# Moving the rounding and the DMAs of fifteen weight tiles inside the first batch of a two-layer kernel

## The chip, the cores and the metric

The kernel runs on one core of a Trainium2 chip. The metric is the device time of one launch in microseconds (us). Before the change it is 2076.19 us, the median of three runs (2070.89 to 2077.12). The engines are TensorE (PE; its weight loads are PEld), VectorE (DVE), ScalarE (ACT), GpSimd (POOL) and SyncE (SP, which only issues DMAs here).

## The reference

Eight sequences of 512 tokens with 256 channels go through two layers. In each, a normalised input feeds an attention and a gated feed-forward net, and their product is added to the input. All is in fp32.

```python
x = L0_attn_x                                   # (8, 512, 256)
xn = _layernorm(x)
s = L0_attn(xn)    # 16 heads of 16, 4 key heads, bias -slope*sqrt(i-j), causal
g = _silu(L0_ffn(xn))                           # silu(x W1') * (x W3'), Walsh-Hadamard, W2'
x = x + s * g
xn = _layernorm(x)
s = L1_attn(xn)    # differential attention, 32 softmaxes of width 8, rms norm
g = _silu(L1_ffn(xn))                           # shared expert and 8 experts of width 176, top 2
x = x + s * g
```

## The kernel before

**Batches and units.** One batch is one sequence; there are B = 8, one after the other. Within a batch, layer 0 is four *units* (u = 0 to 3, four heads each) and layer 1 is eight (u = 4 to 11). A unit goes through eleven *packs* of scores (`SCORE_PACKS`): for each, PE makes the scores (line 535), DVE adds the distance bias to six of the eleven in layer 0 (`dve_bias`, line 812), and ACT takes the exponentials (`act_exps`, line 696). POOL masks and multiplies two of the four heads (`pool_distances`, lines 826 and 829), for key tiles kt = 0, 1, 2 in turn. Then PE multiplies by v (`pe_pv`, line 551).

**The maxima of the next unit.** Between the packs of unit u, PE also makes the scores of unit u + 1 (`pe_max_pack`, lines 501 and 508) and DVE takes their row maxima (`dve_maxima`, lines 794 and 797). When all eleven are done, PE transposes them (line 514), ACT copies them as `mneg` (line 676) and SP writes them into a row of the q ring. `mneg` is the mark by which the prediction counts units.

**Up tiles.** The feed-forward weights come in 22 *up tiles*. Layer 0 uses tiles 0 to 7, layer 1 tiles 8 to 21. For each, PE runs 12 matmuls into two banks (line 452, a gate half and a linear half of 6 each), ACT takes a tanh (line 706), and DVE folds it (`dve_gate_half`, line 837, and `dve_linear_half`, line 847). `TILE_IN` gives the tile that is finished inside a unit and `TILE_AFTER` the one that is finished at its end. The matmuls of a linear half wait until the linear half of the tile before has left its bank (`s_h`). In units 1 and 2 the last six matmuls, four ahead of line 514 and two behind it (`UP_BEHIND`), are such a linear half; the one they wait for is `TILE_IN[u]`, folded by DVE at pack 9. After unit 3 come the down products (line 616).

**Late tiles.** Each weight is used as a sum of two rounded parts: high (rounded to fp32r) and low (the remainder). A rounded tile is kept in the DRAM image `up_img`, from which SP and ACT load it when it is due. Seven tiles are made in a setup block ahead of the batches. The fifteen others, 7 to 21, are made in the first batch only (b = 0), during its four layer-0 units, by the table `LATE_TILES` (4, 4, 4 and 3 tiles). Each goes through four steps in one of four places in SBUF (`late_pairs`, tile t in place (t - 7) mod 4: two in `hbuf`, one in `xn`, one in `x`):

- `pool_late_in` (line 960): POOL issues the load of 256 KB, after the store of the tile that had the place before has landed (`s_lout`);
- `act_late_high` (line 965): ACT rounds, after the load has landed (`s_lin`);
- `dve_late_low` (line 970): DVE subtracts, after the ACT step (`s_lhi`);
- `pool_late_out` (line 976): POOL issues the store of 512 KB into `up_img`, after the DVE step (`s_llo`).

**What sets the order.** It is written out by hand: each engine runs its own program in order (`act_batch`, `dve_batch`, `pool_batch`), and counted semaphores join them. An instruction that waits holds everything behind it on its engine. In the first batch, before the change, ACT and DVE do the roundings of a unit behind all its packs, and POOL issues the loads of a unit's tiles between its kt = 0 and kt = 1 work of that same unit. The tiles of unit 0 are loaded at its start.

Of the kernel before, what the change touches and what calls it, by code (L numbers as in the profile page):

```python
# [36 lines left out]
UNITS = (4, 8)  # L37
# [80 lines left out]
def gated_layers_kernel(nc, x_in, w0_qk, w0_v, w0_o, w_up, w0_down, w1_qk, w1_v, w1_o, w1_down,  # L118
                        w1_gate, gate_bias, lambdas, subln, c_ident, c_hadamard, c_dist, c_causal, out):
    with ExitStack() as ctx:  # L120
# [835 lines left out]
        def pool_late_in(pool, t):  # L956
            n, s = divmod(t - UP_EARLY, LATE_STAGES)
            if n:
                pool.wait_ge(s_lout[s], so_far(s_lout[s], 16 * n))
            nc.gpsimd.dma_start(late_pairs[s][:, 1, :], w_up[t]).then_inc(s_lin[s], 16)  # L960

        def act_late_high(act, t):
            n, s = divmod(t - UP_EARLY, LATE_STAGES)
            act.wait_ge(s_lin[s], so_far(s_lin[s], 16 * (n + 1)))
            nc.scalar.copy(late_pairs[s][:, 0, :].bitcast(F32R), late_pairs[s][:, 1, :]).then_inc(s_lhi, 1)
# [209 lines left out]
        with nc.Block() as block:  # L1175
# [220 lines left out]
            def act_batch(act, b, more_batches):  # L1396
                def unit(u):
                    for i in range(PACKS):
                        if i == PACKS - 1 and u < UNITS[0] - 1:
                            act_max_copy(act, u + 1)  # L1400
                        act_exps(act, u, i)
                        if i == 8 and U0[1] <= u < U_ALL - 1:
                            act_tanh(act, TILE_AFTER[u])
                        if i == PACKS - 1 and U0[1] <= u < U_ALL - 1:
                            act_max_copy(act, u + 1)
                        if i == 1 and u not in U0:
                            act_pv_copy(act, u - 1)
                        if i == 1 and u == 0:
                            act_tanh(act, 0)
                        if i == (4 if u < UNITS[0] - 1 else 6) and u in TILE_IN:  # L1410
                            act_tanh(act, TILE_IN[u])
                        if u == U_ALL - 1 and i in (6, 9) and more_batches:
                            act_turn(act, 0, (6, 9).index(i))
                        if u == U_ALL - 1 and i == 7:
                            act_tanh(act, TILE_AFTER[u])
                    if u < UNITS[0]:
                        act_tanh(act, TILE_AFTER[u])
                    if u < UNITS[0] and not b:
                        for t in LATE_TILES[u]:
                            act_late_high(act, t)  # L1420
                    if u < UNITS[0] - 1:
                        if u:
                            act.wait_ge(s_pm2, so_far(s_pm2, 3 * u))
                        act_strips(act, u + 1)
                    if last_of_layer(u):
                        act_pv_copy(act, u)

                for u in range(UNITS[0]):
                    unit(u)
                act_tanh_down(act, 0, 0)  # L1430
                act_o_turn(act, 0)
                act_turn(act, 1, 0)
                act_tanh_down(act, 0, 1)
                act_turn(act, 1, 1)
                act_project(act, 1, 0)
                act_project(act, 1, 1)
                act.wait_ge(s_rp, so_far(s_rp, 1))
                nc.scalar.activation(rt[:, 0].rearrange("p t e -> p (t e)"), MX[1][:, 0:NT * NE], ACT.Tanh,
                                     scale=0.5).then_inc(s_rsg, 1)
                act_v(act, 1)  # L1440
                act_tanh(act, FRONT_TILES[0])
                act_project(act, 1, 2)
                act_tanh(act, FRONT_TILES[1])
                up_load(act, FRONT_TILES[1] + 2)
                act_project(act, 1, 3)
                act_tanh(act, FRONT_TILES[2])
                up_load(act, FRONT_TILES[2] + 2)
                act.wait_ge(s_rT, so_far(s_rT, 1))
                nc.scalar.copy(gT[:], MISC[0:NE, :]).then_inc(s_rTc, 1)
                act_tanh(act, FRONT_TILES[3])  # L1450
                up_load(act, FRONT_TILES[3] + 2)
                act_max_copy(act, UNITS[0])
                for j in FRONT_TILES[4:]:
                    act_tanh(act, j)
                    up_load(act, j + 2)
                for u in range(UNITS[0], U_ALL):
                    unit(u)
                if not more_batches:
                    act_tanh_down(act, 1, 0)
                    act_o_turn(act, 1)  # L1460
                    act_tanh_down(act, 1, 1)
                    return

                for i in range(3):
                    act_project(act, 0, i)
                act_v(act, 0)
                act.wait_ge(s_rm, so_far(s_rm, 1))
                act_strips(act, 0)
                act_tanh_down(act, 1, 0)
                act_o_turn(act, 1)  # L1470
                act_tanh_down(act, 1, 1)
                act.wait_ge(s_mrow[1], so_far(s_mrow[1], 16 * (U_ALL - 1)))
                act_max_copy(act, 0)
# [7 lines left out]
            def dve_batch(dve, b, more_batches):  # L1481
                def unit(u):
                    more = not last_of_layer(u)
                    late = layer_of(u) == 0
                    for i in range(PACKS):
                        if late and i in BIAS_PACKS and i < PACKS - 1:
                            dve_bias(dve, u, i)
                        if more:
                            dve_maxima(dve, u + 1, i)
                        if i == 1 and u == 0:  # L1490
                            dve_gate_half(dve, 0)
                        if i == 2 and u == 0:
                            dve_linear_half(dve, 0)
                        if late and more and u in TILE_IN and i == 5:
                            dve_gate_half(dve, TILE_IN[u])
                        if late and more and u in TILE_IN and i == 9:
                            dve_linear_half(dve, TILE_IN[u])
                    if u in TILE_IN and not more:
                        dve_gate_half(dve, TILE_IN[u])
                    if late:  # L1500
                        dve_bias(dve, u, PACKS - 1)
                    if u in TILE_IN and not more:
                        dve_linear_half(dve, TILE_IN[u])
                        dve_normalise(dve, u - 1)
                    dve_gate_half(dve, TILE_AFTER[u])
                    dve_linear_half(dve, TILE_AFTER[u])
                    if more and u not in U0:
                        dve_normalise(dve, u - 1)
                    if late and not b:
                        for t in LATE_TILES[u]:  # L1510
                            dve_late_low(dve, t)
                    if last_of_layer(u) and u < U_ALL - 1:
                        dve_normalise(dve, u)

# [100 lines left out]
            def pool_batch(pool, b, more_batches):  # L1615
                for u in range(UNITS[0]):
                    if u == 0 and not b:
                        for t in LATE_TILES[0]:
                            pool_late_in(pool, t)
                        for img in (q_img, k_img):  # L1620
                            nc.gpsimd.dma_start(img[1][:, 3:32:4, :], qring[1][:, 0, 0:2, :].bitcast(F32)).then_inc(s_pad, 16)
                    for kt in range(NT - 1):
                        pool_distances(pool, u, kt)
                        if u and kt == 0 and not b:
                            for t in LATE_TILES[u]:
                                pool_late_in(pool, t)
                    if u == 1 and not b:
                        pool.wait_ge(s_pad, so_far(s_pad, 32))
                        nc.gpsimd.dma_start(k_img[1][3:32:4, 31, :], kring[0][MROW:MROW + 1, 0:1, :].bitcast(F32)
                                            .to_broadcast([1, 8, T])).then_inc(s_ones, 16)  # L1630
                    if not b:
                        for t in LATE_TILES[u]:
                            pool_late_out(pool, t)
                    if u == UNITS[0] - 1 and not b:
                        for l in (0, 1):
                            nc.gpsimd.dma_start(wo[l][:], (w0_o, w1_o)[l]).then_inc(s_wo[l], 16)
# [119 lines left out]
```

## Time and profile before

| what | value |
|---|---|
| median of three runs | 2076.19 us |
| the profiled execution | 2082.67 us |
| its span | 2080.9 us |
| PE, DVE, ACT, POOL busy | 94%, 68%, 42%, 33% |
| first batch, layer 0 | from 54.63 to 124.67 us |
| second batch, layer 0 | from 319.70 to 379.28 us |

The span is the time between the first and the last instruction in the trace; the profiled execution's time is 1.8 us longer. Engine times are counted from the start of the span. A busy share is an average over the whole span and says little about one batch; for the fifteen tiles only the stretch from 54 to 128 us counts, and the second batch, which has the same four units without late tiles, is what it can be held against.

### The profile page before, as it was taken

Reading aid. Unit: us, or ns where it says so; the run is one execution under the profiler, and the core shown is the slowest. Engines: PE = TensorE matmul, PEld = TensorE weight load, DVE = VectorE, ACT = ScalarE, POOL = GpSimd, SP = SyncE. Lnnn points to the kernel's source line nnn. Section 1 sums busy time; section 2 is a strip of 40 time slices with the busy share of each in tenths; the row PEclk is TensorE's granted clock in tenths of the full one; section 3 lists DMA queues with packets and bytes.
Section 4 is the critical chain, followed back from the end, with each engine's and each line's share of the span. In section 5 each row is a group of like instructions: output and inputs, shape, how many; then the busy total and the mean of one; then the engine's idle time right before and its main releaser. Section 6 shows DMA issues by size and latency. Waiting matters only on the chain.

```text
span 2080.9 us, 33061 instructions
## 1 busy us (share of the span) xinstructions
PE 1955.8 (94%) x11618; PEld 1434.5 (69%) x11618; DVE 1406.1 (68%) x3474; ACT 880.2 (42%) x1753; POOL 683.5 (33%) x846
## 2 busy tenths in 40 slices
PE   5889999999999999999999999999999989999998
PEld 3566676766767667686676766767677766767666
DVE  6847758477575775757766676666766567675773
ACT  3534624345252452515524264243543436333462
POOL 2633413243142441414414143133332334232341
PEclk8999999999999999999999999999999999999999
DMA  8647332262322524234242442415332163421630
GB/s 265 213 144 245 100 101 61 72 208 83 102 77 97 172 73 118 71 128 147 63 112 81 161 128 64 106 63 185 118 89 68 62 200 115 103 61 42 204 101 16
DMA packets 105261, 240.46 MB, mean 116 GB/s; under 512 B 16700, under 2 KB 26940, under 8 KB 104840
## 3 DMA queue, kind: packets, MB, share of 16 engines
q1 hardware_dynamic: 85080, 173.44, 27.8%
q0 software_dynamic: 14256, 43.94, 6.8%
q10 hardware_dynamic: 5760, 20.97, 3.0%
q8 instruction: 93, 1.52, 0.3%
q14 instruction: 72, 0.59, 0.1%
HBM read 179.67 MB, written 57.82 MB: 114 GB/s over the span
## 4 chain that ended last, share of the span: by engine, by line
PE 75%; DVE 12%; DMA 5%; issue 3%; ACT 1%; POOL 1%; DVEq 0%; ACTq 0%; POOLq 0%; SPq 0%
PE bank L452 22%; PE bank L616 15%; PE bank L535 11%; PE bank L501 11%; PE bank L551 8%; DVE bank L794 4%; DMA qring<-mneg 4%; PE bank L637 3%; DVE nmax L797 3%; PE bank L508 2%; PE bank L561 2%; PE bank L514 1%; DVE probs L812 1%; PE bank L463 1%; DVE xn L746 1%
## 5 line engine op out<-in xcount | busy, mean ns | idle before, releaser
L452 PE MATMUL bank<-xnT,upring 128*128 128x512 f32 (+1 forms) x2208 | 713.5, 405 | 1.4 <-DVE hbuf L837 1.4
L794 DVE CUSTOM_DVE_ANT_0 bank<-bank,mask_strip 128x512 f32<-128x512 f32 (+1 forms) x768 | 479.0, 635 | 197.6 <-PE bank L501 195.6
L696 ACT ACTIVATE probs<-bank 128x512 f32<-128x512 f32 (+1 forms) x720 | 388.2, 555 | 282.8 <-PE bank L535 256.6
L452 PEld LDWEIGHTS bank<-xnT,upring 128*128 128x128 f32 x2208 | 405.4, 194 | 60.4 <-DVE hbuf L837 9.2
L501 PE MATMUL bank<-kring,qring 127*128 127x128 f32 (+3 forms) x1280 | 379.5, 350 | 23.0 <-DVE nmax L794 14.7
L535 PE MATMUL bank<-qring,kring 128*128 128x512 f32 (+1 forms) x880 | 358.2, 411 | 40.8 <-DMA qring<-mneg 19.3
L616 PE MATMUL bank<-wdown,hbuf 128*128 128x256 f32 x1408 | 324.4, 380 | 0.0
L501 PEld LDWEIGHTS bank<-kring,qring 127*128 127x128 f32 x1280 | 227.1, 193 | 114.5 <-DVE nmax L794 62.6
L616 PEld LDWEIGHTS bank<-wdown,hbuf 128*128 128x128 f32 x1408 | 263.4, 190 | 35.5 <-issue 1.7
L535 PEld LDWEIGHTS bank<-qring,kring 128*128 128x128 f32 x880 | 169.1, 194 | 128.8 <-issue 44.9
L1662 POOL TENSOR_SCALAR_AFFINE_SELECT probs<-probs 128x512 f32<-128x512 f32 x200 | 128.3, 642 | 369.1 <-ACT probs L696 368.7
L797 DVE TENSOR_REDUCE nmax<-bank 128x2 f32<-128x512 f32 (+1 forms) x288 | 199.0, 691 | 51.7 <-PE bank L508 42.9
L551 PE MATMUL bank<-probs,v 128*17 128x384 f32 (+3 forms) x2368 | 207.3, 452 | 4.1 <-POOL probs L829 3.6
L837 DVE SCALAR_TENSOR_TENSOR hbuf<-tb,bank 128x512 f32<-128x512 f32 x176 | 120.2, 683 | 88.9 <-ACT tb L706 88.9
L826 POOL TENSOR_SCALAR_AFFINE_SELECT probs<-probs 128x256 f32<-128x256 f32 x64 | 26.6, 416 | 421.0 <-ACT probs L696 421.0
L847 DVE SCALAR_TENSOR_TENSOR hbuf<-hbuf,bank 128x512 f32<-128x512 f32 x176 | 120.6, 685 | 28.0 <-PE bank L452 15.0
L829 POOL TENSOR_TENSOR probs<-probs,shared 128x1024 f32<-128x1024 f32 x64 | 135.7, 2121 | 5.3
L706 ACT ACTIVATE tb<-bank 128x512 f32<-128x512 f32 x176 | 104.3, 593 | 74.9 <-PE bank L452 74.9
L696 ACT ACTIVATE probs<-probs 128x512 f32<-128x512 f32 (+1 forms) x160 | 93.6, 587 | 91.2 <-DVE probs L812 91.2
L551 PEld LDWEIGHTS bank<-probs,v 128*17 128x17 f32 x2368 | 57.6, 97 | 102.7 <-issue 73.3
L1602 POOL TENSOR_TENSOR hbuf<-hbuf,gring 128x512 f32<-128x512 f32 x88 | 113.7, 1292 | 33.2 <-DMA gring<-gate_img 28.7
L713 ACT ACTIVATE tb<-bank 128x512 f32<-128x512 f32 x32 | 19.1, 597 | 244.2 <-PE bank L616 244.2
(165 smaller groups left out, 2309.4 us busy)
## 6 DMA issues: line engine op xcount, KB each, us to landing
upring<-up_img SPq DMA_DIRECT2D x136, 512.0 KB, 4.0
upring<-up_img ACTq DMA_DIRECT2D x40, 512.0 KB, 5.6
q_img<-probs SPq DMA_DIRECT2D x32, 512.0 KB, 3.3
kring<-k_img SPq DMA_DIRECT2D x64, 256.0 KB, 3.0
qring<-q_img SPq DMA_DIRECT2D x32, 384.0 KB, 4.7
qring<-q_img SPq DMA_DIRECT2D x192, 64.0 KB, 2.0
q_img<-probs SPq DMA_DIRECT2D x32, 256.0 KB, 4.0
k_img<-probs SPq DMA_DIRECT2D x16, 512.0 KB, 5.7
```

Of the source, the lines that this page charges most:

```text
L452: last = nc.tensor.matmul(out_ap, part_a(a, pa, k), part_b(b, pb, k), start=(n == 0), stop=(n == len(steps) - 1))
L501: last = nc.tensor.matmul(bk[:, (g - g0) * w:(g - g0 + 1) * w], q_of(u)[0:MROW, g, qt * P:(qt + 1) * P], k_of(u)[0:MROW, 0:w], start=True, ...
L535: nc.tensor.matmul(SC[n % 2][:, 0:heads * w].rearrange("p (g n) -> p g n", g=heads), k_of(u)[:, kt * P:(kt + 1) * P], q_of(u)[:, g0:g0 + h ...
L551: last = nc.tensor.matmul(PV[32 * g:32 * g + DV + 1, kt * P:T], v[l][:, kt, hv, :], probs_of(u, kt)[:, g, :], start=(kt == 0), stop=(kt == ...
L616: last = nc.tensor.matmul(FB[tt // 2][:, (tt % 2) * C:(tt % 2 + 1) * C], hbuf[:, j, tt * P:(tt + 1) * P], wdown[l][:, j, :], start=(j == 0 ...
L696: nc.scalar.activation(pr, pr if biased else scores, ACT.Exp, scale=scale).then_inc(s_exp, 1)
L794: nc.vector.tensor_tensor_reduce(scores, scores, mask_strip[:, T - w:T], 1.0, -BIG, ALU.add, ALU.max, nmax[:, u % 2, g0, qt:qt + 1]).then_ ...
L797: nc.vector.tensor_reduce(nmax[:, u % 2, g0:g0 + heads, qt], MX[n % 2][:, 0:heads * w].rearrange("p (g n) -> p g n", g=heads), AX.X, ALU.m ...
L829: nc.gpsimd.tensor_tensor(pr[:, :, 0:w], pr[:, :, 0:w], estrip[:, u % 2, :, 0:w], ALU.mult).then_inc(s_pm2, 1)
L837: nc.vector.scalar_tensor_tensor(hbuf[:, layer_tile(j)[1], :], tb[:], 1.0, FB[0][:], ALU.add, ALU.mult).then_inc(s_gu, 1)
L847: nc.vector.scalar_tensor_tensor(h, h, 0.5, FB[1][:], ALU.mult, ALU.mult).then_inc(s_h, 1)
L1662: nc.gpsimd.affine_select(pr, pr, [[0, G4], [1, P]], ALU.is_ge, 0.0, base=0, channel_multiplier=-1).then_inc(s_pm, 1)
```

## The change

Only the first batch is touched. The same fifteen loads, roundings and stores are done, in the same places in SBUF.

- ACT: in unit u, the k-th late tile is rounded right behind the exponentials of pack 5 + k, and no longer behind the unit.
- DVE: the k-th late tile is subtracted right behind the maxima of pack 6 + k, and no longer behind the unit.
- POOL: the stores of unit u stay behind its kt = 2 work, and the loads for unit u + 1 follow them at once, ahead of the kt = 0 work of unit u + 1. Before, they stood behind that work.

```diff
@@ act_batch, unit(u)
                         act_exps(act, u, i)
+                        if u < UNITS[0] and not b and 5 <= i < 5 + len(LATE_TILES[u]):
+                            act_late_high(act, LATE_TILES[u][i - 5])
...
                     if u < UNITS[0]:
                         act_tanh(act, TILE_AFTER[u])
-                    if u < UNITS[0] and not b:
-                        for t in LATE_TILES[u]:
-                            act_late_high(act, t)
@@ dve_batch, unit(u)
                         if more:
                             dve_maxima(dve, u + 1, i)
+                        if late and not b and 6 <= i < 6 + len(LATE_TILES[u]):
+                            dve_late_low(dve, LATE_TILES[u][i - 6])
...
                     if more and u not in U0:
                         dve_normalise(dve, u - 1)
-                    if late and not b:
-                        for t in LATE_TILES[u]:
-                            dve_late_low(dve, t)
@@ pool_batch
                     for kt in range(NT - 1):
                         pool_distances(pool, u, kt)
-                        if u and kt == 0 and not b:
-                            for t in LATE_TILES[u]:
-                                pool_late_in(pool, t)
...
                     if not b:
                         for t in LATE_TILES[u]:
                             pool_late_out(pool, t)
+                        if u < UNITS[0] - 1:
+                            for t in LATE_TILES[u + 1]:
+                                pool_late_in(pool, t)
```

DVE in unit 1, packs 7 to 10, before the change (L812 is a bias, L794 and L797 are maxima, L847 the linear half of tile 2):

```order
L812 SCALAR_TENSOR_TENSOR probs<-dist,bank 128x384
L794 ISA bank,nmax<-bank,mask_strip 128x384
L794 ISA nmax 128x1
L797 TENSOR_REDUCE nmax<-bank 128x2
L812 SCALAR_TENSOR_TENSOR hbuf<-dist,bank 128x256 x2
L797 TENSOR_REDUCE nmax<-bank 128x2
L847 SCALAR_TENSOR_TENSOR hbuf<-hbuf,bank 128x512
L797 TENSOR_REDUCE nmax<-bank 128x4
```

The same place on DVE after the change, from the end of pack 6 (L970 is the subtraction of a late tile):

```order
L970 TENSOR_TENSOR hbuf<-hbuf 128x512
L812 SCALAR_TENSOR_TENSOR probs<-dist,bank 128x384
L794 ISA bank,nmax<-bank,mask_strip 128x384
L794 ISA nmax 128x1
L970 TENSOR_TENSOR hbuf<-hbuf 128x512
L797 TENSOR_REDUCE nmax<-bank 128x2
L970 TENSOR_TENSOR xn<-xn 128x512
L812 SCALAR_TENSOR_TENSOR hbuf<-dist,bank 128x256 x2
L797 TENSOR_REDUCE nmax<-bank 128x2
L970 TENSOR_TENSOR x<-x 128x512
L847 SCALAR_TENSOR_TENSOR hbuf<-hbuf,bank 128x512
L797 TENSOR_REDUCE nmax<-bank 128x4
```

All four subtractions now stand ahead of the linear half and of the last maxima of the unit; units 0 and 2 have the same pattern.

POOL between units 2 and 3 before the change (L976 stores, L960 loads, L826 and L829 the two steps of `pool_distances`):

```order
L976 DMA up_img<-hbuf 128x1024 x2
L976 DMA up_img<-xn 128x1024
L976 DMA up_img<-x 128x1024
L826 AFFINE_SELECT probs<-probs 128x2x128
L829 TENSOR_TENSOR probs<-probs,shared 128x1024
L960 DMA hbuf<-in_w_up 128x512 x2
L960 DMA xn<-in_w_up 128x512
L826 AFFINE_SELECT probs<-probs 128x2x128
L829 TENSOR_TENSOR probs<-probs,shared 128x2x384
```

And after it:

```order
L976 DMA up_img<-hbuf 128x1024 x2
L976 DMA up_img<-xn 128x1024
L976 DMA up_img<-x 128x1024
L960 DMA hbuf<-in_w_up 128x512 x2
L960 DMA xn<-in_w_up 128x512
L826 AFFINE_SELECT probs<-probs 128x2x128
L829 TENSOR_TENSOR probs<-probs,shared 128x1024
L826 AFFINE_SELECT probs<-probs 128x2x128
L829 TENSOR_TENSOR probs<-probs,shared 128x2x384
```

The loads, each of which waits for a store to land, have moved from between kt = 0 and kt = 1 to ahead of both.

## Rows read from the trace of the kernel before

**Rows 1.** The page's first line.

```profile
span 2080.9 us, 33061 instructions
```

**Rows 2.** Chain of waits, 50 to 160 us: start, us, what.

```profile
106.56 6.49 DMA up_img<-hbuf
...
115.67 1.81 POOL probs L829
```

**Rows 3.** PE by 1 us: length, busy (instructions), granted clock, DMA share, GB/s.

```profile
116.00:117.00 1.00, 0.00 (x0) 0.67 0.98 397
...
122.00:123.00 1.00, 1.00 (x3) 0.50 0.00 0
123.00:124.00 1.00, 1.00 (x8) 0.92 0.00 0
```

**Rows 4.** ACT, the mneg copies, first batch, then second: start, us, instruction, [idle before].

```profile
68.00 0.27 ACT L676 ACTIVATE mneg<-bank 16x128 fp32r<-16x128 f32 x1 [1.10 <-PE bank L514]
...
84.68 0.27 ACT L676 ACTIVATE mneg<-bank 16x128 fp32r<-16x128 f32 x1 [1.95 <-PE bank L514]
...
101.66 0.27 ACT L676 ACTIVATE mneg<-bank 16x128 fp32r<-16x128 f32 x1 [1.93 <-PE bank L514]
...
333.69 0.27 ACT L676 ACTIVATE mneg<-bank 16x128 fp32r<-16x128 f32 x1 [1.42 <-PE bank L514]
...
348.50 0.27 ACT L676 ACTIVATE mneg<-bank 16x128 fp32r<-16x128 f32 x1 [1.93 <-PE bank L514]
...
363.75 0.27 ACT L676 ACTIVATE mneg<-bank 16x128 fp32r<-16x128 f32 x1 [1.92 <-PE bank L514]
```

**Rows 5.** PE at the end of unit 3, first batch, then second.

```profile
117.62 1.48 PE L551 MATMUL bank<-probs,v 128*17 128x384 f32 x8 [3.62 <-POOL probs L829]
119.03 4.93 PE L452 MATMUL bank<-xnT,upring 128*128 128x512 f32 x12
...
124.67 3.72 PE L616 MATMUL bank<-wdown,hbuf 128*128 128x256 f32 x16
...
375.54 3.04 PE L452 MATMUL bank<-xnT,upring 128*128 128x512 f32 x12
...
379.28 3.72 PE L616 MATMUL bank<-wdown,hbuf 128*128 128x256 f32 x16
```

**Rows 6.** DVE, the late subtractions behind unit 0.

```profile
71.00 1.28 DVE L970 TENSOR_TENSOR hbuf<-hbuf 128x512 fp32r<-128x512 f32 x2
...
73.41 0.69 DVE L794 CUSTOM_DVE_ANT_0 bank<-bank,mask_strip 128x512 f32<-128x512 f32 x1
```

**Rows 7.** DVE at the end of unit 1's packs.

```profile
82.58 0.68 DVE L847 SCALAR_TENSOR_TENSOR hbuf<-hbuf,bank 128x512 f32<-128x512 f32 x1
83.18 0.68 DVE L797 TENSOR_REDUCE nmax<-bank 128x4 f32<-128x512 f32 x1
```

**Rows 8.** Waits, 54 to 128 us: engine, line, for whom: total, times, longest.

```profile
PEld bank L452 <- DVE hbuf L847: 0.8, 2, 0.4
```

**Rows 9.** DVE and PE in unit 0.

```profile
64.79 0.69 DVE L797 TENSOR_REDUCE nmax<-bank 128x2 f32<-128x512 f32 x1 [0.75 <-PE bank L508]
...
66.16 1.48 DVE L797 TENSOR_REDUCE nmax<-bank 128x2 f32<-128x512 f32 x2
...
67.69 0.28 PE L514 MATMUL bank<-ident,nmax 128*16 128x128 f32 x1
```

**Rows 10.** Loads (line 960), then stores (line 976): time from issue to landing.

```profile
DMA to landing us min/median/max: 3.1/4.4/5.4
...
DMA to landing us min/median/max: 3.4/6.3/8.2
```

**Rows 11.** ACT and POOL, end of unit 2 and unit 3.

```profile
97.79 0.58 ACT L696 ACTIVATE hbuf<-bank 128x512 f32<-128x512 f32 x1
...
109.23 0.85 ACT L696 ACTIVATE probs<-bank 128x384 f32<-128x384 f32 x2
...
105.95 1.15 POOL L976 DMA_DIRECT2D up_img<-hbuf  x2 [3.36 <-DVE hbuf L970]
```

## The prediction, made before the changed kernel was run

> **What bounds the kernel now.** The page's head gives the span, 2080.9 us [rows 1]. The profiled execution took 2082.67 us, 6.5 us above the median of the three runs, 2076.19; I sum against the profiled execution and carry the difference over to the median unchanged. What the measurement can tell from no change is about 0.3%, 6.2 us.
>
> I then set the first batch's layer 0 beside the second's, which does the same work without late tiles. The marks are the copies of mneg, one per unit, and the start of the down products. From the mneg of unit 0 to that of unit 1 it is 84.68 - 68.00 = 16.68 us in the first batch and 348.50 - 333.69 = 14.81 in the second; to that of unit 2 it is 16.98 against 15.25 [rows 4]. From there to the down products it is 124.67 - 101.66 = 23.01 against 379.28 - 363.75 = 15.53 [rows 4, 5]. So the late tiles cost 1.87 + 1.73 + 7.48 = 11.1 us behind the first mneg. That is the most that this change could give back, 0.53% of the launch.
>
> The 7.48 us are read from the chain of waits. It goes through a store of unit 2's tiles for 6.49 us and then to POOL's kt = 1 work, which starts at 115.67 [rows 2]. POOL issues unit 3's loads between kt = 0 and kt = 1, each load waits for a store, and so kt = 1 is late: PE idles 3.62 us for it [rows 5]. Behind the idle time the granted clock falls to one half, 1.2 of 2.4 GHz, at about 116.3 (a third of that microsecond is at the old level), and comes back at about 123.2 [rows 3]. The twelve matmuls in it take 4.93 us against 3.04 in the second batch [rows 5]. The rest is shorter waits of the same kind, and the subtractions that still run when unit 3 starts.
>
> **The change part by part.**
>
> *Subtractions on DVE, units 0 to 2.* Four take 73.41 - 71.00 = 2.41 us [rows 6], 0.60 each. They go away behind the unit, where the next unit's first maxima now start as soon as PE has them, as in the second batch. They come in ahead of the unit's last maxima. In unit 1 DVE runs its last rows back to back, 82.58 and 83.18 [rows 7], and PE's weight loads for tile 3's linear half already wait for the linear half of tile 2 on DVE, 0.4 us each time [rows 8]. Both stand behind all four subtractions now, so line 514 and the mneg move by the full 2.41 us. Unit 1 is then the second batch's 14.81 + 2.41 = 17.22 us, 0.54 more than before. Unit 2 is 15.25 + 2.41 = 17.66, 0.68 more. The change loses there: more is put into the packs than leaves the seam, since of the 2.41 us only 1.87 and 1.73 were ever on the path there, the rest ran while PE was busy anyway.
>
> In unit 0 DVE has slack: it idles 0.75 us at 64.79 and the last two maxima end at 66.16 + 1.48 = 67.64 [rows 9]. With the four subtractions that is 67.64 + 2.41 - 0.75 = 69.3, less some 0.2 us of small gaps, 69.1. Line 514 was at 67.69 [rows 9] and is then 1.4 us later, so the first mneg is at 69.4. Bounds for the 2.41 us in the packs: nothing, if PE has other work wherever DVE is late; or 4 x (0.6 + 0.7) = 5.2, if every rounding on ACT and its subtraction run one after the other with DVE standing. I take 2.41, since ACT waits for DVE in front of most of its packs and so is ready first.
>
> *POOL.* The stores need only the last subtraction and kt = 2. In unit 2 the exponentials of pack 8 were at 97.79 [rows 11]; I put them at some 98.5 (its packs start half a microsecond earlier, and two subtractions stand ahead). POOL's kt = 2 is a little shorter than its kt = 1, whose multiplication alone is 1.81 us [rows 2]; with 2 us for it, the stores go out from about 101 in place of 105.95 [rows 11]. A store lands 6.3 us after its issue in the median and a load 4.4 us [rows 10]. Unit 3's loads are then issued from 107.3 and the first is in at 111.7. ACT wants it after pack 5: mneg of unit 2 at 104.3 (below) plus what that took before, 109.23 + 0.85 - 101.66 = 8.4, less the 0.9 us that this stretch lost to the subtractions, 111.8. So it is just in time. POOL's kt = 0 starts at about 109, close to where it was, but kt = 1 follows it at once, by about 112 and long before PE wants it. The 3.62 us and the fall of the clock go. For the loads of units 1 and 2 there is more room, since ACT wants them seven microseconds into the unit and the stores leave at the end of the unit before.
>
> The Trainium skill (DMA: Bandwidth & Descriptors, section on the anatomy of one DMA on the SWDGE path) fits a GpSimd-issued transfer with 2.0 us plus the bytes at 436 KB per us. My estimate from that page for three stores in flight is 2.0 + 3 x 1.2 = 5.6 us, a little shorter than the row's median, and would leave the forecast as it is.
>
> *Queued behind the new waits.* On POOL the waits for landed stores now hold kt = 0 too, for which PE waits at the seventh pack of unit 3. On ACT the wait for a load holds the exponentials of packs 6 to 8, and with them PE's next scores. SP issues the same transfers in the same order; its loads of tiles 7 and on wait for stores that land earlier than before. The last three stores and the output weights leave POOL earlier too and are wanted only in the down products.
>
> *Unit 3.* It takes no maxima, so DVE and ACT have idle time. Three subtractions are 1.8 us; between nothing and all of it is lost, I take half, 0.9 us. From mneg to down products that is 15.53 + 0.9 = 16.43 in place of 23.01, 6.58 less.
>
> **Sum.** mneg of unit 0 at 68.00 + 1.4 = 69.4; unit 1 at 69.4 + 17.22 = 86.6; unit 2 at 86.6 + 17.66 = 104.3; down products at 104.3 + 16.43 = 120.7, against 124.67. In terms: +1.4 + 0.54 + 0.68 - 6.58 = -4.0 us. Nothing behind moves against the down products. The span becomes 2076.9, the profiled execution 2078.7, the median 2072.2.
>
> **The rivals.**
>
> *A: the packs hide more.* If half of the 2.41 us is hidden in units 0 to 2, 3 x 1.2 = 3.6 us more come back: 7.6 in all, 2068.6. For it: PE runs a pack ahead of DVE and has up matmuls to fill in. Against it: rows 7 and 8 show no room at the end of units 1 and 2.
>
> *B: the transfers are late.* With the slowest store and load, 8.2 and 5.4 us [rows 10], unit 3's first load is in at 101 + 13.6 = 114.6, and ACT stands 2.8 us. The gain is 1.2 us, 2075.0. For it: these slowest ones were in this very stretch, with SP's loads beside them. Against it: the stores now go out before SP's loads.
>
> *C, the other side: the clock falls in units 1 and 2.* PE has run out of up matmuls at the end of the packs and now waits about 2 us for the linear half and the last maxima, with shorter waits ahead. If the granted clock then halves in both units for as long as it did in rows 3, 123.2 - 116.3 = 6.9 us, and PE has work throughout, each costs half of that, 3.4 us. The sum is -4.0 + 6.8: slower by 2.8 us, 2079.0. It decides from about 2 us per unit on. For it: rows 3 show such a fall. Against it: there PE stood for 3.62 us, and here it has work ahead of the wait and behind it. The Trainium skill (TensorE: Matmul & The Clock Gate, section on what's actually happening) says that the clock follows how busy TensorE has been of late; by that, several waits could add up to what one long one does, and rival C would be likelier than the single row makes it.
>
> *D: nothing moves.* The orders of the engines do change, so this needs gains and losses to cancel by chance, 2076.2; it lies between B and C.
>
> **How the numbers follow.** Forecast with its neighbourhood (gain 2.5 to 5.5 us) 0.5; A 0.17; B and D 0.21; C 0.12. The measured medians scatter: the three runs shown lie 6 us apart, which is half as much again as the forecast gain. The range reaches from A to between B and C, with a microsecond of scatter: 2067.5 to 2077.5; only C and the far end of A are left out. Faster by over 0.3% needs 6.2 us, so A or good luck in the medians: 0.21. Slower by over 0.3% needs worse than C: 0.04. Within 0.3%: 0.75.
>
> **What would show it.** In the profile after: mneg at about 69.4, 86.6 and 104.3 and down products at about 120.7; periods of units 1 and 2 half a microsecond longer than before; no wait of PE for POOL's line 829 in unit 3, and full clock from there to the down products; stores of unit 2's tiles from about 101; waits of ACT's line 965 for loads near zero. The forecast is wrong if the periods of units 1 and 2 shrink (A), if ACT or POOL stand for DMAs in unit 3 by more than a microsecond (B), or if the clock drops between 84 and 108 us (C).

## The result: slower, 2086.24 us against the 2072.2 forecast

| | before | after |
|---|---|---|
| median, 5 runs each on one chip | 2074.19 us (2070.89 to 2077.12) | 2086.24 us (2083.35 to 2092.51) |
| ratio | | 1.0065 [1.0051, 1.0079] |
| the profiled execution | 2082.67 us | 2089.81 us |
| first batch's layer 0, first scores to down products | 70.04 us | 80.87 us |

The loss lies in the stretch that was changed (the last row of the table; *stretch* stands for it from here on): 10.8 us more there, against 12 us in the medians. Behind the down products the profiled execution takes 1952.2 us, where before takes 1956.2; over all the profiles below this part lies between 1947.8 and 1960.8 us, so a profile is compared by its stretch, and a launch by its median. Each kernel has one profile, the kernel before a second one, with a stretch of 68.86 us in place of 70.04; differences of a microsecond between stretches say nothing.

The copies of mneg on ACT in the kernel after, the rows that answer to [rows 4]:

```profile
70.66 0.27 ACT L676 ACTIVATE mneg<-bank 16x128 fp32r<-16x128 f32 x1 [1.82 <-PE bank L514]
...
94.18 0.27 ACT L676 ACTIVATE mneg<-bank 16x128 fp32r<-16x128 f32 x1 [3.20 <-PE bank L514]
...
115.60 0.27 ACT L676 ACTIVATE mneg<-bank 16x128 fp32r<-16x128 f32 x1 [2.83 <-PE bank L514]
```

Unit 1 takes 23.52 us in place of 16.68 and unit 2 21.42 in place of 16.98; 17.22 and 17.66 were forecast. Unit 3 is shorter than before, but not by what was forecast:

```profile
122.25 0.47 PE L535 MATMUL bank<-qring,kring 128*128 128x512 f32 x1 [3.51 <-DMA qring<-mneg]
...
132.14 3.05 PE L452 MATMUL bank<-xnT,upring 128*128 128x512 f32 x12 [0.48 <-DVE hbuf L837]
```

This is PE in unit 3 after, and answers to [rows 5]: the twelve matmuls take 3.05 us, so the clock is whole, and no wait for POOL's line 829 stands in the unit. In its place stands a wait that did not exist before, at the unit's first scores, for the row of maxima that SP writes from mneg (line 426). PE's waits of after, 54 to 137 us, from the same view as [rows 8], show what is new:

```profile
PE bank L535 <- DMA qring<-mneg: 8.1, 3, 3.5
...
PE bank L535 <- DVE probs L812: 4.2, 5, 1.2
PE bank L452 <- DVE hbuf L847: 3.8, 2, 1.9
```

**The first cause: the row of maxima is late.** It is 8 KB. Before, it landed 1.8 us after its issue in all three units; PE had the last packs' products with v to do meanwhile and never waited. Line 426 before:

```profile
DMA to landing us min/median/max: 1.8/1.8/1.8
```

From the chain of waits of after:

```profile
70.96 5.61 DMA qring<-mneg
...
94.47 5.19 DMA qring<-mneg
...
115.89 6.22 DMA qring<-mneg
```

What moved ahead of it stands in POOL's rows of after:

```profile
69.08 1.14 POOL L976 DMA_DIRECT2D up_img<-hbuf  x2
70.20 0.55 POOL L976 DMA_DIRECT2D up_img<-xn  x1
70.72 0.54 POOL L976 DMA_DIRECT2D up_img<-x  x1
72.53 0.55 POOL L960 DMA_DIRECT2D hbuf<-in_w_up  x1 [1.27 <-DMA up_img<-hbuf]
```

```profile
up_img<-x POOLq DMA_DIRECT2D x1, 512.0 KB, 6.1
```

The last row is of the DMA view of 69 to 79 us (size, us to landing). The four stores of 512 KB are issued in the two microseconds ahead of the row. The last of them lands at 70.72 + 6.1 = 76.8, and the row at 76.57, together with it. In units 1 and 2 it is the same: last store 99.5 and 121.9, row 99.66 and 122.11. Before, they stood behind the unit's roundings and so always behind the row. The Trainium skill (DMA: Bandwidth & Descriptors, section on queues, rings and completion order) has the DMA engines take turns between the queues packet by packet; by that alone a small row on SP's queue should wait for little more than a packet. The rows above show more than that: the row arrives only with the last of the 2 MB. The same section of the Trainium skill says that the write which signals a transfer's end lands only after every earlier write of its DMA engine, across its queues. This could hold the row back as well; no run here tells whether its data or its signal is late.

**The second cause: the subtraction stands while POOL works.** DVE, then POOL, in unit 1 of after:

```profile
85.27 1.63 DVE L970 TENSOR_TENSOR hbuf<-hbuf 128x512 fp32r<-128x512 f32 x1
87.77 0.68 DVE L970 TENSOR_TENSOR hbuf<-hbuf 128x512 fp32r<-128x512 f32 x1
88.97 0.67 DVE L970 TENSOR_TENSOR xn<-xn 128x512 fp32r<-128x512 f32 x1
90.83 0.98 DVE L970 TENSOR_TENSOR x<-x 128x512 fp32r<-128x512 f32 x1
```

```profile
84.52 1.84 POOL L829 TENSOR_TENSOR probs<-probs,shared 128x768 f32<-128x768 f32 x1
89.00 0.91 POOL L826 TENSOR_SCALAR_AFFINE_SELECT hbuf<-hbuf 128x256 f32<-128x256 f32 x1 [2.65 <-ACT hbuf L696]
90.00 1.27 POOL L829 TENSOR_TENSOR hbuf<-hbuf,shared 128x512 f32<-128x512 f32 x1
```

POOL's multiplication ends at 84.52 + 1.84 = 86.36 and the first subtraction at 86.90, 0.54 later. The next one of POOL ends at 91.27 and the last subtraction at 91.81, again 0.54 later. So DVE does next to nothing of these subtractions, which take 0.68 us alone, before POOL is done. It goes the other way too: POOL's line 826 at 89.00 takes 0.91 in place of 0.41 us, and a subtraction has begun just before it, at 88.97. The Trainium skill (SBUF — State Buffer, section on the two separate sides) states this rule: a DVE operation with two inputs in SBUF and a GpSimd operation that reads SBUF take one pair of ports in turn, each for its whole length. The trace agrees: all seven subtractions that start while POOL computes end 0.54 to 0.55 us behind it. The biases with one operand in a bank keep their length: the one of 128x384 at 84.33, under POOL's multiplication, takes 0.55 us, and the one at 86.83, with POOL idle, 0.54.

**The clock** falls twice between the marks of units 0 and 2: at about 76.1, in the 3.34 us that PE stands for the row, and at about 93.2, less than 1 us behind PE's wait of 1.88 us for tile 2's linear half. PE by 1 us in after, columns as in [rows 3]:

```profile
75.00:76.00 1.00, 0.00 (x0) 1.00 1.04 240
76.00:77.00 1.00, 0.30 (x1) 0.57 1.03 361
77.00:78.00 1.00, 1.00 (x3) 0.50 0.90 320
...
93.00:94.00 1.00, 1.00 (x5) 0.61 1.02 410
94.00:95.00 1.00, 1.00 (x4) 0.50 0.88 328
```

**What they add up to.** The stretches of after, mneg to mneg: length, busy time of each engine, granted clock.

```profile
55.03:70.66 15.63, 12.99 (x41) 8.34 (x43) 14.81 (x34) 7.91 (x15) 12.31 (x15) 0.78 0.52 180
70.66:94.18 23.52, 17.02 (x87) 10.73 (x87) 16.94 (x40) 10.82 (x22) 12.71 (x17) 0.91 0.63 193
94.18:115.60 21.42, 16.97 (x91) 10.51 (x92) 17.00 (x39) 10.70 (x22) 11.52 (x14) 0.94 0.55 198
115.60:135.90 20.30, 15.20 (x110) 8.32 (x108) 11.80 (x23) 11.18 (x22) 12.48 (x15) 1.00 0.67 238
```

Unit 1 is 6.30 us over its forecast: 3.34 for the row, 0.95 + 0.30 for two subtractions that stand (1.63 and 0.98 against 0.68), and 0.09 x 23.52 = 2.1 by the clock, 6.7 in all. Unit 2 is 3.76 over: 1.27 for the row, some 1.2 again for two subtractions, and 0.06 x 21.42 = 1.3. Unit 3 is 3.87 over, 3.51 of it for the row. These sums are read from one trace; the experiments test them.

### The profile page after: what moved, and what is told of

Same layout as the page of the kernel before. It is cut to its first block, busy times and chain, and to the rows that moved or that the text cites. A ratio compares the mean times of both kernels' runs of the same rounds, so it can differ in the third digit from the quotient of the medians.

```text
span 2088.1 us, 32972 instructions
## 1 busy us (share of the span) xinstructions
PE 1952.5 (94%) x11529; PEld 1431.8 (69%) x11618; DVE 1410.3 (68%) x3474; ACT 879.9 (42%) x1753; POOL 684.8 (33%) x846
## 4 chain that ended last, share of the span: by engine, by line
PE 74%; DVE 13%; DMA 5%; issue 3%; ACT 1%; POOL 1%; ACTq 0%; DVEq 0%; POOLq 0%; SPq 0%
PE bank L452 22%; PE bank L616 15%; PE bank L535 10%; PE bank L501 9%; PE bank L551 8%; DMA qring<-mneg 4%; DVE bank L794 4%; PE bank L508 4%; DVE nmax L797 3%; PE bank L637 3%; PE bank L561 2%; PE bank L514 1%; DVE probs L812 1%; PE bank L463 1%; DVE xn L746 1%
## 5 line engine op out<-in xcount | busy, mean ns | idle before, releaser
L794 DVE CUSTOM_DVE_ANT_0 bank<-bank,mask_strip 128x512 f32<-128x512 f32 (+1 forms) x768 | 478.5, 634 | 206.2 <-PE bank L501 204.2
L797 DVE TENSOR_REDUCE nmax<-bank 128x2 f32<-128x512 f32 (+1 forms) x288 | 198.7, 690 | 48.5 <-PE bank L508 39.7
L826 POOL TENSOR_SCALAR_AFFINE_SELECT probs<-probs 128x256 f32<-128x256 f32 x64 | 26.5, 414 | 427.8 <-ACT probs L696 427.8
L829 POOL TENSOR_TENSOR probs<-probs,shared 128x1024 f32<-128x1024 f32 x64 | 136.9, 2138 | 5.3
L847 DVE SCALAR_TENSOR_TENSOR hbuf<-hbuf,bank 128x512 f32<-128x512 f32 x176 | 120.5, 685 | 26.5 <-PE bank L452 13.4
L706 ACT ACTIVATE tb<-bank 128x512 f32<-128x512 f32 x176 | 104.3, 592 | 69.6 <-PE bank L452 69.6
L812 DVE SCALAR_TENSOR_TENSOR probs<-dist,bank 128x128 f32<-128x128 f32 (+2 forms) x256 | 105.4, 446 | 27.8 <-PE bank L535 27.2
```

What stands on the lines that cost most here:

```text
L794: nc.vector.tensor_tensor_reduce(scores, scores, mask_strip[:, T - w:T], 1.0, -BIG, ALU.add, ALU.max, nmax[:, u % 2, g0, qt:qt + 1]).then_ ...
L797: nc.vector.tensor_reduce(nmax[:, u % 2, g0:g0 + heads, qt], MX[n % 2][:, 0:heads * w].rearrange("p (g n) -> p g n", g=heads), AX.X, ALU.m ...
L812: last = nc.vector.scalar_tensor_tensor(probs_of(u, kt)[:, g, :], dist[:, 0:w], -SLOPES[4 * u + g] / EXP_SCALE[0], SC[n % 2][:, (g - g0) * ...
L829: nc.gpsimd.tensor_tensor(pr[:, :, 0:w], pr[:, :, 0:w], estrip[:, u % 2, :, 0:w], ALU.mult).then_inc(s_pm2, 1)
L847: nc.vector.scalar_tensor_tensor(h, h, 0.5, FB[1][:], ALU.mult, ALU.mult).then_inc(s_h, 1)
```

## The experiments

**Row first.** POOL waits for the row to land before it issues the stores.

```diff
+                        if u < UNITS[0] - 1:
+                            pool.wait_ge(s_mrow[1], so_far(s_mrow[1], 16 * (u + 1)))
                         for t in LATE_TILES[u]:
                             pool_late_out(pool, t)
```

> The changed kernel, but in units 0 to 2 POOL waits for the landing of the next unit's maxima row before it issues the unit's stores. Theory 1 (the 8 KB row lands 5.2 to 6.2 us after its issue in place of 1.8 because the stores were issued just ahead of it and fill the DMA engines): the row lands in 1.8 us again, PE's waits of 3.3 to 3.5 us for it go, with the low clock behind the first; about 10 us faster than the changed kernel, near 2076 us or level with the kernel before. Rival (the row is late for another reason, and the in-pack roundings on DVE are what costs): the row stays late or its landing is not worth more than 3 us, time above 2082 us.

Measured: 2102.39 us against 2077.0, ratio 1.0121 [1.0099, 1.0144]; stretch 93.90 us. The row is back to 1.8 us in every unit, and yet this is the slowest kernel of all, 26 us above its expectation. Stores that leave later make the loads behind them late, and these hold ACT, five times and 18.0 us in all, and behind ACT PE, inside the packs:

```profile
81.81 0.62 ACT L965 CAST hbuf<-hbuf 128x512 fp32r<-128x512 f32 x1 [5.41 <-DMA hbuf<-in_w_up]
```

The expectation took it that the loads had room. They have none: with the roundings in the packs, stores, loads and row all want the same few microseconds between two units. The granted clock is low for much of this too, 0.83, 0.76 and 0.75 in units 1 to 3.

**Roundings alone.** The loads go back behind the kt = 0 work.

```diff
                         pool_distances(pool, u, kt)
+                        if u and kt == 0 and not b:
+                            for t in LATE_TILES[u]:
+                                pool_late_in(pool, t)
...
-                        if u < UNITS[0] - 1:
-                            for t in LATE_TILES[u + 1]:
-                                pool_late_in(pool, t)
```

> The changed kernel with the loads back behind kt = 0 of their own unit; the stores leave as early as in the changed kernel. Theory 1 (stores delay the row): row still lands after 4 to 6 us and the time stays within 4 us of the changed kernel's 2086. Rival (the loads that follow at once are what the row queues with): row back near 1.8 us and 8 us or more faster than the changed kernel.

Measured: 2097.34 us, ratio 1.0093 [1.0076, 1.0110]; stretch 87.04 us. The row's landing, over the three units, with no load issued near it:

```profile
DMA to landing us min/median/max: 4.0/5.1/5.2
```

So it is in the main the stores that delay it; the loads behind them, which after has and this kernel has not, add 0.4 to 1.2 us in the same unit. The time missed its expectation, 2082 to 2090 us: the loads come late for ACT, which stands 6.7 us for four of them, and the clock reads 0.81, 0.89 and 0.80 in units 1 to 3.

**POOL's order alone.** The opposite half: the kernel before with the loads moved, the roundings left behind the units.

```diff
-                        if u and kt == 0 and not b:
-                            for t in LATE_TILES[u]:
-                                pool_late_in(pool, t)
...
+                        if u < UNITS[0] - 1:
+                            for t in LATE_TILES[u + 1]:
+                                pool_late_in(pool, t)
```

> The kernel before with only POOL's order of the change: unit u+1's loads right behind the stores of unit u, ahead of kt = 0. ACT and DVE round behind the unit as before. Theory 1 (early stores delay the row): stores still leave after the row has landed, row 1.8 us, but POOL's kt = 0 to 2 stand behind landed stores, so PE waits for POOL at the end of units 1 and 2 (about 2 us each) and in unit 3 (about 6 us); slower than the kernel before by 6 to 10 us. Rival (POOL's order is harmless by itself): within 2 us of the kernel before.

Measured: 2084.7 us, ratio 1.0038 [1.0025, 1.0051]; stretch 72.40 us. The row takes 1.8 us, as it must where the stores follow it. Units 2 and 3 are worse, 18.37 us in place of 16.98 and 24.60 in place of 23.01. The largest wait is in unit 3, where POOL's work now stands behind three waits for stores:

```profile
118.19 1.91 PE L551 MATMUL bank<-probs,v 128*17 128x512 f32 x8 [6.68 <-issue]
```

The end of POOL's kt = 0 work, 118.10, releases these products. The stretch accounts for 2.4 to 3.5 of the 7.7 us by which the median is worse; the runs do not show where the rest lies. Neither half of the change is a gain by itself.

**Small transfers.** Stores of the fifteen tiles are cut to 64 KB, and the loads of tiles 7 to 21 into the up ring with them. The rest of those weights is left out of the computation.

```diff
+            c = 2 * T if j < UP_EARLY else 128
-            sp.dma_start(upring[...]...bitcast(F32), up_img[j])\
+            sp.dma_start(upring[...]...bitcast(F32)[:, 0:c], up_img[j][:, 0:c])\
...
-            nc.gpsimd.dma_start(up_img[t], late_pairs[s].rearrange("p a n -> p (a n)"))
+            nc.gpsimd.dma_start(up_img[t][:, 0:128], late_pairs[s].rearrange("p a n -> p (a n)")[:, 0:128])
```

> The changed kernel with 64 KB of each late tile stored in place of 512 KB, and 64 KB of tiles 7 to 21 loaded from the image in all batches (the rest of those weights is left out). Same instructions, waits and order. Theory 1 (the stores ahead of it in the DMA engines delay the maxima row): the row lands after about 2 us, PE's three waits for it (8.1 us in the trace of the changed kernel) and the half clock behind them go; the first batch's layer 0, 80.9 us in the changed kernel, becomes about 70 us. Rival (the row is late because SP or the row's own issue is late, or the time lies in the packs): row and stretch within 2 us of the changed kernel's. What is left over the 59.6 us of the second batch is the roundings inside the packs.

Measured: 2078.62 us against 2078.3, ratio 1.0003 [0.9992, 1.0014]; stretch 74.44 us, 6.4 less than after and 4.4 above its expectation. The median cannot be held against before in the same way, since the loads of tiles 7 to 21 are smaller in all eight batches. The row's landing:

```profile
DMA to landing us min/median/max: 1.8/3.5/3.5
```

The small stores land so soon that in units 1 and 2 the 256 KB loads now leave just ahead of the row. PE has no wait for it any more. The subtractions still stand, up to 2.38 us.

**A narrow multiplication.** POOL's kt = 1 multiplication runs over 8 columns of each head in the first batch; that of the other columns is left out.

```diff
+            if kt == 1 and not batch[0]:
+                w = 8
```

> The changed kernel with POOL's multiplication of kt = 1 cut to 8 columns in the first batch (the distance factor of two heads is left out there). Theory 2 (a subtraction on DVE that reads two SBUF operands stands still while POOL runs an operation in SBUF): the first subtraction of each unit takes 0.68 us again in place of 1.63 to 1.78, and the stretch of the first batch's layer 0 falls by 3 to 4 us. Rival (the long subtraction waits for something else, as ACT's rounding): it stays above 1.5 us.

Measured: 2087.81 us, ratio 1.0046 [1.0030, 1.0062]; stretch 77.28 us, 3.6 less than after. DVE's subtractions in it (their line is 972 there), with the shortest, median and longest in ns:

```profile
L972 DVE TENSOR_TENSOR hbuf<-hbuf x8: 683/685/715, 61.8 to 123.6; 128x512 fp32r<-128x512 f32 x8
L972 DVE TENSOR_TENSOR xn<-xn x4: 680/680/693, 64.6 to 125.0; 128x512 fp32r<-128x512 f32 x4
L972 DVE TENSOR_TENSOR x<-x x3: 993/997/1023, 66.4 to 107.2; 128x512 fp32r<-128x512 f32 x3
```

In after the first of these rows reads 678/1158/1779. The third is unchanged, since kt = 2 was not narrowed. Only POOL's work has changed, on data that these subtractions do not touch, so the standing is a matter of the two engines at once. PE's waits stay:

```profile
PE bank L535 <- DMA qring<-mneg: 8.9, 3, 3.4
```

DVE has 1.10 + 0.95 + 0.95 + 1.08 = 4.1 us less to do in the four units. What of the stretch's 3.6 us this is worth stays open: by the granted clock (0.78, 0.91, 0.94 and 1.00 in the units of after; 0.89, 1.00, 1.00 and 0.92 here) the low clock cost 6.8 us of full clock there and 3.3 here. The median is no proof of a gain either: the ratios of this kernel and of after, 1.0046 and 1.0065, have intervals that overlap.

**Stores inside the packs.** A full version that tries to mend the row: roundings two packs sooner, stores between POOL's kt = 1 and kt = 2 work, loads behind it.

```diff
-                        if u < UNITS[0] and not b and 5 <= i < 5 + len(LATE_TILES[u]):
-                            act_late_high(act, LATE_TILES[u][i - 5])
+                        if u < UNITS[0] and not b and 3 <= i < 3 + len(LATE_TILES[u]):
+                            act_late_high(act, LATE_TILES[u][i - 3])
...
+                        if kt == 1 and not b:
+                            for t in LATE_TILES[u]:
+                                pool_late_out(pool, t)
```

> The changed kernel with ACT's roundings two packs earlier (3 to 6), DVE's subtractions at packs 4 to 7, and POOL's stores between kt = 1 and kt = 2; the loads for the next unit stay behind kt = 2. The stores are then landed or nearly so when the maxima row is issued. Theory 1: row 1.8 to 3 us, PE's waits for it under 1 us each, the first batch's layer 0 about 71 to 73 us; time about 2077, level with the kernel before, since DVE still does 2.4 us and more of subtractions inside each unit's packs. Rival (subtractions in the packs are the whole loss): no better than the changed kernel by more than 3 us.

Measured: 2090.71 us, ratio 1.0056 [1.0039, 1.0074]; stretch 77.47 us. The expectation was 71 to 73 us, with the row at 1.8 to 3. The row takes 3.8, 4.7 and 5.2 us, now with loads issued just ahead of it and the last store still on its way (in unit 1 it lands at 87.37 + 5.5 = 92.9, and the row is issued at 91.22), and PE waits 6.0 us for it. Shifting the burst forward only brings its other half into the row's way.

**Both causes out.** Small transfers as above, loads of the late tiles cut to 32 KB too, and the kt = 1 and kt = 2 multiplications narrow. The same parts of the computation are left out as in the two kernels above, and more of them.

```diff
+            if kt and not batch[0]:
+                w = 8
...
-            nc.gpsimd.dma_start(late_pairs[s][:, 1, :], w_up[t])
+            nc.gpsimd.dma_start(late_pairs[s][:, 1, 0:64], w_up[t][:, 0:64])
```

> The changed kernel with both disputed costs taken away: stores of 64 KB and loads of 32 KB of each late tile in place of 512 and 256 KB (and 64 KB of tiles 7 to 21 loaded from the image in all batches), and POOL's multiplications of kt = 1 and 2 cut to 8 columns in the first batch (weights and distance factors are left out so far). If row and standing subtractions are all that the prediction missed, what is left is what it summed: periods of 17.2 and 17.7 us for units 1 and 2 and a stretch of 66 us from the first scores to the down products, against 80.9 in the changed kernel; the row lands in 1.8 us and all subtractions take 0.68 us. If something else was missed, the periods stay above 19 us.

Measured: 2073.69 us against 2076.71, ratio 0.9981 [0.9968, 0.9994]; stretch 66.14 us. Its stretches, mneg to mneg, and the row's landing:

```profile
53.26:67.88 14.62, 11.66 (x41) 7.90 (x43) 13.48 (x34) 7.80 (x15) 10.35 (x17) 0.88 0.38 128
67.88:85.09 17.21, 15.26 (x87) 9.55 (x87) 15.58 (x40) 10.82 (x22) 9.92 (x16) 1.00 0.38 87
85.09:102.74 17.65, 15.72 (x91) 10.05 (x91) 15.74 (x39) 10.70 (x22) 9.43 (x17) 1.00 0.28 86
102.74:119.40 16.66, 15.20 (x110) 8.31 (x108) 10.86 (x23) 11.18 (x22) 7.91 (x13) 1.00 0.21 59
```

```profile
DMA to landing us min/median/max: 1.9/2.2/2.8
```

All subtractions take 0.68 to 0.75 us. The median has the lighter loads of tiles 7 to 21 in all eight batches in it, as with small transfers; the stretch has them only in unit 3. The forecast had 14.77, 17.22, 17.66 and 16.43, together 66.1. With the two causes gone the kernel does, in units 1 to 3, what the prediction's sum said. In unit 0 the agreement is in part luck: the forecast started from 13.37 us, the longest of five profiles that have the same unit 0 (the shortest 12.08), and its clock read 0.74, against 0.88 here. The two causes together, with the clock that fell behind them, are worth 80.87 - 66.14 = 14.7 us. Taken out alone they give back 6.4 and 3.6 us; the other 4.7 come only when both are out. Part of that is the clock, 1.00 in units 1 to 3 here but 0.92 in unit 3 of each single one (and in unit 2 of small transfers), part may be the row's 3.5 us, which small stores alone left, and part what only this kernel leaves out (smaller loads, the kt = 2 multiplication). How the 4.7 divides was not measured.

**Unit 3's loads alone.** The kernel before, with one thing changed: in unit 3 the three loads stand behind the kt = 1 work.

```diff
-                        if u and kt == 0 and not b:
+                        if u and kt == (1 if u == UNITS[0] - 1 else 0) and not b:
```

> The kernel before, but in unit 3 the three loads stand behind kt = 1 in place of kt = 0; all else as before. The rows of the kernel before say that PE's 3.62 us wait for kt = 1, the shorter waits ahead of it and the half clock behind it go: gain 5.5 to 6 us, about 2069. Rival (the loads then come too late for ACT's roundings and push the copy of the PV product): ACT waits for the loads ahead of that copy by more than 3 us and the gain is under 2 us.

Measured: 2074.26 us (10 runs) against 2077.0, ratio 0.9990 [0.9979, 1.0002]; stretch 62.71 us, the shortest so far, but launches that could not tell it from no change. Since its stretch was 7 us shorter, it was run again, beside the kernel before once more:

> The kernel before, unchanged, for a second profile. If PE's 3.6 us wait for POOL in unit 3 and the half clock behind it belong to the program, they are there again and the first batch's layer 0 is 68 to 71 us; if they hang on the phase of the clock or on luck with the stores, it is 64 to 67 us. This says how much unit3_loads_late, whose trace is 7.3 us shorter in this stretch and whose median is only 2 to 3 us lower, could have gained.

Measured: 2077.06 us in the one run, stretch 68.86 us, with PE's 3.0 us wait for POOL's line 829 in it again. And the version:

> unit3_loads_late once more, unchanged, with more rounds. Its trace is 6.2 to 7.3 us shorter in the first batch's layer 0 than the two traces of the kernel before, while its median was 2 to 3 us lower (interval of the ratio 0.9979 to 1.0002). If the gain is real, the ratio is 0.997 with 1 outside the interval; if it is given back later in the launch, 0.999 to 1.000.

Measured: 2070.24 us (12 runs, 2067.94 to 2073.34) against 2076.71 (23 runs), ratio 0.9973 [0.9963, 0.9983]; stretch 62.45 us. The two studies' intervals overlap only from 0.9979 to 0.9983; a gain of about 0.2% is what both allow. POOL, then PE, in unit 3 of it:

```profile
109.25 1.84 POOL L829 TENSOR_TENSOR probs<-probs,shared 128x768 f32<-128x768 f32 x1
111.03 1.14 POOL L960 DMA_DIRECT2D hbuf<-in_w_up  x2
112.15 0.54 POOL L960 DMA_DIRECT2D xn<-in_w_up  x1
```

```profile
111.50 0.84 PE L551 MATMUL bank<-probs,v 128*17 128x384 f32 x8
...
115.99 3.72 PE L616 MATMUL bank<-wdown,hbuf 128*128 128x256 f32 x16
```

kt = 1 is done at 111.1, the stores have landed by the time POOL comes to the loads, and PE waits for neither: the products that in [rows 5] take 1.48 us behind 3.62 idle take 0.84 behind none. ACT stands for one load, 0.7 us. Units 1 and 2 are as before, 16.66 and 16.98, and unit 3 takes 16.73 in place of 23.01. That is 6.28 us, where the change hoped for 6.58 in this unit, at the price of moving three DMA issues. This kernel beats both.

## Why the prediction was wrong, step by step

- *"SP issues the same transfers in the same order"*: this is the step that failed. The sentence is true of SP and misses the point: POOL's stores moved past SP's row in time. The prediction moved the stores' issue from behind to ahead of mneg's copy and asked only when the stores and loads would land, never what small transfer would land behind them. Priced at nothing; PE waited 8.1 us for it.
- *Four subtractions at 0.60 us each*: mis-sized. The duration came from [rows 6], behind the unit, where POOL issues DMAs and computes nothing. In the packs two of four start while POOL computes, at 1.63 to 1.78 and 0.98 us. Some 1.2 us a unit.
- *Line 514 and mneg move by the full 2.41 us in units 1 and 2*: right once the two causes are out (17.21 and 17.65 us). So the sum of the seam (the time between two units) against the packs was sound, and the change would have lost there in any case.
- *Unit 0 later by 1.4 us*: too little. 15.63 in after and 14.62 with the causes out, against 14.77; but unchanged unit 0 took 12.08 to 13.37 us in five profiles, so with the causes out it is 1.3 to 2.5 us later, and the total of 66.14 against 66.1 owes something to that.
- *The 3.62 us and the clock's fall in unit 3 go*: right. Unit 3 took 20.30 us, and without the row's 3.51 that is 16.8 against 16.43 forecast. But the step was credited to the whole change, while unit 3's loads alone bring it, by POOL's order in one unit.
- *Stores from about 101*: 113.00 in after. In before's time that is unit 2's mneg less 2.6 us, as against 3.3 forecast, so the shift within the unit was right and the lateness is that of the units ahead.
- *Rival B* (late transfers): the loads that it feared were no matter in after, where ACT waits for none, but count in the row-first kernel, where ACT stands up to 6.6 us for one.
- *Rival C* (the clock in units 1 and 2): its sign, a fall between 84 and 108 us, did come, at 93.2. The low clock cost 2.1 + 1.3 = 3.4 us in the two units against the 6.8 of the rival, and a part of it stands behind the row's wait, which the rival did not have. The wait for the linear half does not suffice as the reason: PE waits 1.89 us for it in unit 2 of after and in both units of the narrow kernel, and the clock reads 1.00 behind it each time. What more it takes the runs do not show.
- Rivals A and D never came near. No rival held the mechanism that decided, and the chance of 0.04 for slower by over 0.3% came from them alone. The range ended at 2077.5, 9 us short.

## What to carry to other kernels

When bulk transfers are moved, list every small transfer that will be issued in the microseconds behind them, on any queue, and ask who waits for it; an 8 KB row that nobody waited for became the longest wait of the stretch. A duration is worth what its neighbour was doing: take a two-operand DVE instruction's price from a row where GpSimd computes, if it will stand beside GpSimd. And before many things are moved to cure one wait, move the one thing that the wait names.

## What the runs showed of the hardware

- An 8 KB write on SP's queue took 1.8 us from issue to landing with no bulk transfer issued in the 3 us ahead of it, 5.2 to 6.2 us behind four GpSimd-issued stores of 512 KB, with GpSimd-issued loads following (4.0 to 5.2 us without them), and 3.5 us behind 64 KB stores and 256 KB loads.
- A DVE subtraction with both inputs in SBUF, 128x512, took 0.68 us alone. Seven times in after it started while GpSimd computed, and it ended 0.54 to 0.55 us after that instruction: 1.63 to 1.78 us beside the longer one, 0.98 beside the shorter. A GpSimd select of 0.41 us took 0.91 just behind the start of such a subtraction, and a multiplication of 1.84 us took 2.39.
- PE idled 3.51 us at 118.7 to 122.2 in after and the granted clock stayed at 1.00; it idled 3.34 us up to 76.70 and the clock went to 0.50 (1.2 of 2.4 GHz). In both places it had run 16 + 8 + 8 products with v just ahead. In the narrow kernel it idled 3.35 us in the same place, up to 74.49, and the clock stayed at 1.00. What told these apart the runs do not show.
